# Last layer: picks 16 buffers ahead, rows brought back straight into their place, additions of four tiles; mixer: a unit's gates in one instruction

## The reference, cut to what matters

```python
x = x + 0.5 * ffn(layernorm(x), gate_w, experts)
x = x + mixer(layernorm(x), ...)
x = x + 0.5 * ffn(layernorm(x), gate_w, experts)

def ffn(x, gate_w, experts):                      # E = 8 experts, M = N // E = 256 tokens each
    gates = sinkhorn(einsum('bnd,de->bne', x, gate_w))          # 8 iterations
    vals, idx = top_k(swapaxes(gates, -1, -2), M)               # each expert picks its 256 tokens
    routed = x[b_idx, idx]                                      # (e, b, m, d)
    out = einsum('ebmd,edf->ebmf', routed, experts) * vals
    return zeros_like(x).at[b_idx, idx].set(out)                # the last expert that picked a token wins

def mixer(x, ...):      # inner = 512 channels, 16 states each
    x_ssm, res = split(x @ W_in.T)
    xc = silu(conv(x_ssm) + conv_b); delta = softplus(xc)
    h_t = exp(delta_t * A) * h_{t-1} + xc_t * xc_t              # a scan over 2048 tokens
    return (xc * sum(h) * silu(res) + D * xc) @ W_out.T
```

## Time and profile before

| | us |
|---|---|
| median of 3 runs | 3703.75 |
| lowest and highest run | 3695.53, 3709.73 |
| the profiled execution: its own time | 3714.21 |
| its span | 3712.6 |
| last stage (ffn), from 3294 us to the end | 418.6 |
| mixer, about 330 to 2950 us | 2620 |
| busy over the span: DVE, PE, ACT, POOL | 3117.0, 2790.2, 2127.8, 1321.5 |

### The profile page before, as it was taken

How to read it: one execution, slowest core, us unless ns; L and a number is a source line. 1 busy time by engine, 2 the same in 40 slices (tenths; PEclk the granted TensorE clock), 3 DMA queues, 4 the chain that set the end, 5 groups by cost and what they waited for, 6 DMA issues and landing times. The chain is left out here.

```text
span 3712.6 us, 29747 instructions
## 1 busy us (share of the span) xinstructions
PE 2790.2 (75%) x9252; PEld 1532.0 (41%) x9252; DVE 3117.0 (84%) x2640; ACT 2127.8 (57%) x2285; POOL 1321.5 (36%) x894
## 2 busy tenths in 40 slices
PE   8702688889889889988978978998897796035553
PEld 4501343345346345434534634543452455024442
DVE  6797479999999999999999999999999667982222
ACT  5300467876877877688687787778767362001111
POOL 0002265346245344534624534460111100036665
PEclk9655799999899899999989989998998896567776
DMA  6202278688778878867877787885676571034666
GB/s 265 117 0 80 68 174 182 142 174 181 156 167 165 178 163 179 193 134 170 182 161 170 160 178 162 175 193 119 126 150 132 113 283 81 0 117 145 206 220 241
DMA packets 146178, 575.61 MB, mean 155 GB/s; under 512 B 22096, under 2 KB 73872, under 8 KB 99216
## 3 DMA queue, kind: packets, MB, share of 16 engines
q0 software_dynamic: 76704, 400.61, 51.9%
q1 hardware_dynamic: 69360, 173.68, 12.6%
HBM read 154.72 MB, written 119.60 MB: 74 GB/s over the span
## 5 line engine op out<-in xcount | busy, mean ns | idle before, releaser
L1182 DVE TENSOR_TENSOR_SCAN state<-state,drive 128x2048 f32<-128x2048 f32 x512 | 2224.3, 4404 | 51.5 <-ACT state L1388 51.0
L1388 ACT ACTIVATE state<-delta,neg_a 128x2048 f32<-128x2048 f32 x512 | 1019.5, 2005 | 208.0 <-DMA delta<-xc 83.3
L1639 PE MATMUL ps_states<-state,ident 128*128 128x512 f32 x1792 | 847.5, 618 | 81.2 <-DMA state<-state 64.0
L1067 POOL DMA_DIRECT2D state<-state x255 | 235.7, 926 | 1306.1 <-DVE state L1182 1286.8
L1541 PE MATMUL ps_proj<-x1t,w_in 128*128 128x512 f32 x1024 | 515.9, 650 | 92.2 <-ACT res L1337 33.7
L1639 PEld LDWEIGHTS ps_states<-state,ident 128*128 128x128 f32 x1792 | 345.1, 198 | 481.4 <-issue 381.0
L1557 PE MATMUL ps_proj<-conv_in,tap 128*128 128x512 f32 x1024 | 487.8, 627 | 56.6 <-ACT conv_in L1301 35.3
L996 POOL DMA_INDIRECT picked<-normed_rows,slot_now x112 | 355.1, 3170 | 100.9 <-PE ps_rows L1522 56.0
L1541 PEld LDWEIGHTS ps_proj<-x1t,w_in 128*128 128x128 f32 x1024 | 207.2, 207 | 379.0 <-issue 276.7
L1012 POOL DMA_INDIRECT x<-routed_rows,row_now x112 | 344.2, 3074 | 34.8 <-issue 34.8
L1557 PEld LDWEIGHTS ps_proj<-conv_in,tap 128*128 128x128 f32 x1024 | 204.0, 202 | 321.7 <-issue 280.5
(11 more groups left out here) (298 smaller groups left out, 3253.1 us busy)
## 6 DMA issues: line engine op xcount, KB each, us to landing
state<-state POOLq DMA_DIRECT2D x255, 1024.0 KB, 7.1
delta<-xc POOLq DMA_DIRECT2D x24, 1024.0 KB
normed_rows<-rows_in SPq DMA_DIRECT2D x8, 2048.0 KB
x_rows<-x SPq DMA_DIRECT2D x16, 1024.0 KB, 7.7
normed_rows<-rows_mid SPq DMA_DIRECT2D x8, 2048.0 KB
f_total<-x_rows SPq DMA_DIRECT2D x8, 2048.0 KB
routed_rows<-f_routed SPq DMA_DIRECT2D x128, 128.0 KB
out<-f_total SPq DMA_DIRECT2D x8, 2048.0 KB
```

The costliest lines, as they stand in the source:

```text
L1067: nc.gpsimd.dma_start(out=state[held(q)][:], in_=state[held(q - 1)][:], accum_op=ALU.add).then_inc(pair_landed(b, q // 2)[0], 16)
L1182: nc.vector.tensor_tensor_scan(state[held(q)][:], state[held(q)][:], drive[j % 2][:], 0.0, ALU.mult, ALU.add).then_inc(state_ready, 1)
L1388: nc.scalar.activation(state[held(q)][:], delta[j % 2][:], ACT.Exp, scale=g.neg_a[:, j, n:n + 1]).then_inc(decay_ready, 1)
L1639: mm = nc.tensor.matmul(ps_sum[c][:], g.ident[:], state[held(q)][:, c * CH:(c + 1) * CH], start=(opening and n == 1), stop=(n == N - 1))
```

## The change

In `ffn`:

- NX and NY are 16 instead of 8. Picks and brought tiles take their indices from `slot_token` and `token_row` directly; the copies and the waits around them are gone.
- Brought tiles land in `rows`, two buffers of a whole batch (16 tiles), and wait for no addition. The first of a batch waits for the output store of two batches before and, as before, for the batch's 16 stores.
- Of brought tiles 4 go out per 5 picks (`rows_due`), from slot 23 on; what is left follows the last pick.
- DVE adds four tiles in one instruction (GROUP = 4), into `rows`, which is then stored. `added` counts groups.
- SP loads the experts one at a time, those from the third on after a turned slot each, then x of batch 0; x of batch 1 at slot 16; later ones behind the output store of two batches before (which starts five slots after a batch's last brought tile is due), without waiting for it to land. The last batch's output is stored in four parts.
- PE waits for each expert by itself.

In `mixer`: the four PSUM banks are one tensor; a unit's gates are one DVE instruction, 128x2048, for all units but the last; and three of the seven early picks go out after the first pair of the first batch instead of before it.

```diff
@@ mixer
-    ps_sum = [ps(f"ps_states{c}") for c in range(C)]
+    ps_states = ctx.enter_context(nc.psum_tensor("ps_states", [P, NT], F32))
+    ps_sum = [ps_states[:, c * CH:(c + 1) * CH] for c in range(C)]
...
-                for s in range(NX + 4 - FIRST_FFN):
+                for s in range(NX + 1):
                     pick(b + 1, s)
...
                     nc.gpsimd.dma_start(out=state[held(q)][:], in_=state[held(q - 1)][:], accum_op=ALU.add
                                         ).then_inc(pair_landed(b, q // 2)[0], 16)
+                if first and q == 1:
+                    for s in range(NX + 1, NX + 4):
+                        pick(b + 1, s)
...
-            for c in range(C):
-                if last:
-                    dve.wait_ge(end_summed, c + 1)
+            if not last:
+                nc.vector.tensor_tensor(gate_of[j][:], ps_states[:], gate_of[j][:], ALU.mult).then_inc(gated, C)
+            for c in range(C if last else 0):
+                dve.wait_ge(end_summed, c + 1)
@@ ffn
-    NX = NY = NK = 8
+    NX = NY = SL
     NT4 = 4
-    BRING, JOIN, LOAD = SL + 6, SL + 10, 3
+    GROUP = 4
+    NG = T // GROUP
+    BRING, STEP = SL + 6, 5
+
+    def rows_due(n):
+
+        return T * NB if n >= NB * SL else max(0, (n - BRING) * (STEP - 1) // STEP)
+
+    def slot_of(m):
+
+        return next(n for n in range(NB * SL + 1) if rows_due(n) >= (m + 1) * T)
...
-    back = [sb(f"f_back{i}", [P, D]) for i in range(NK)]
+    rows = [sb(f"f_rows{i}", [P, T, D]) for i in range(2)]
...
+        def load_x(m):
+            if m >= 2:
+                sp.wait_ge(added, (m - 1) * NG)
+            sp.dma_start(total[m % 2][:], x_v[m]).then_inc(x_in[m % 2], 16)
+
+        def store_out(m):
+            sp.wait_ge(added, (m + 1) * NG)
+            sp.dma_start(out_v[m], rows[m % 2][:]).then_inc(out_stored[m % 2], 16)
+
+        inside = [m for m in range(NB) if slot_of(m) + 5 < NB * SL]
         for e in range(E):
-            sp.dma_start(expert[:, e, :, :], g.experts[e].rearrange("(k p) f -> p k f", p=P)).then_inc(expert_in, 16)
+            if e >= 2:
+                sp.wait_ge(turned, (e - 2) * NH + 1)
+            sp.dma_start(expert[:, e, :, :], g.experts[e].rearrange("(k p) f -> p k f", p=P)).then_inc(expert_in[e], 16)
         load_x(0)
-        load_x(1)
-        rounds(turn)
...
+        for n in range(NB * SL):
+            b, s = n // SL, n % SL
+            sp.wait_ge(scaled, n + 1)
+            sp.dma_start(routed_v[b][s // NH, 1 + s % NH * P:1 + (s % NH + 1) * P, :],
+                         routed[s % NY][:]).then_inc(routed_out[s % NY], 16)
+            if n == SL:
+                load_x(1)
+            for m in inside:
+                if n == slot_of(m) + 5:
+                    store_out(m)
+                    load_x(m + 2)
+        for m in range(len(inside), NB - 1):
+            store_out(m)
+            if m + 2 < NB:
+                load_x(m + 2)
+        for q in range(NG):
+            sp.wait_ge(added, (NB - 1) * NG + q + 1)
+            sp.dma_start(out_v[NB - 1, :, q * GROUP:(q + 1) * GROUP, :],
+                         rows[(NB - 1) % 2][:, q * GROUP:(q + 1) * GROUP, :]).then_inc(out_stored[(NB - 1) % 2], 16)
...
+        def pick(b, s):
+            pool.wait_ge(turned, count(b * SL + s - NX + 1))
+            pool.sem_inc(g.passed_pool, 1)
+            nc.gpsimd.indirect_dma_start(
+                out=picked[s % NX][:], out_offset=None, in_=g.normed,
+                in_offset=bass.IndirectOffsetOnAxis(ap=g.slot_token[:, b, s:s + 1].bitcast(U32), axis=0)
+            ).then_inc(picked_in[s % NX], 16)
+
+        def bring(m, t):
+            if m == 0 and t == 0:
+                pool.wait_ge(table.ranked, 1)
+            if t == 0:
+                pool.wait_ge(out_stored[m % 2], m // 2 * 16)
+                for k in range(NY):
+                    pool.wait_ge(routed_out[k], (m + 1) * 16 * (SL // NY))
+            pool.sem_inc(g.passed_pool, 1)
+            nc.gpsimd.indirect_dma_start(
+                out=rows[m % 2][:, t, :], out_offset=None, in_=g.routed[m],
+                in_offset=bass.IndirectOffsetOnAxis(ap=g.token_row[:, m, t:t + 1].bitcast(U32), axis=0)
+            ).then_inc(back_in[m % 2][t // GROUP], 16)
+
+        for n in range(NB * SL):
+            pick(n // SL, n % SL)
+            for v in range(rows_due(n), rows_due(n + 1)):
+                bring(v // T, v % T)
...
+        def add_group(v):
+            m, q = v // NG, v % NG
+            part = slice(q * GROUP, (q + 1) * GROUP)
+            if q == 0:
+                dve.wait_ge(x_in[m % 2], (m // 2 + 1) * 16)
+            dve.wait_ge(back_in[m % 2][q], (m // 2 + 1) * 16 * GROUP)
+            nc.vector.tensor_tensor(rows[m % 2][:, part, :], rows[m % 2][:, part, :], total[m % 2][:, part, :], ALU.add
+                                    ).then_inc(added, 1)
+
+        def groups_due(n):
+
+            return rows_due(n - 2) // GROUP
...
-                if s == 1 and isinstance(b, int):
-                    pe.wait_ge(expert_in, E * 16)
+                if s and (s - 1) % NH == 0 and isinstance(b, int):
+                    pe.wait_ge(expert_in[(s - 1) // NH], 16)
```

More of the change, by code:

```diff
@@ L1845, in turn @@
                     dve.wait_ge(table.ranked, 1)
-                if s == 2 and there(b + 1):
-                    set_slots(b + 1)
-                m, t = behind(b, s, JOIN)
-                if there(m):
-                    if t == 0:
-                        dve.wait_ge(x_in[m % 2], (m // 2 + 1) * 16)
-                    dve.wait_ge(back_in[t % NK], (m * (T // NK) + t // NK + 1) * 16)
-                    nc.vector.tensor_tensor(total[m % 2][:, t, :], total[m % 2][:, t, :], back[t % NK][:], ALU.add
-                                            ).then_inc(added, 1)
-                if s == RANKED + 1 and there(b):
-                    set_rows(b)
-        set_slots(0)
         split_tokens(nc, g, dve, table)
-        rounds(turn)
+        for b in range(NB):
+            slots(b)
+        for v in range(groups_due(NB * SL), NB * NG):
+            add_group(v)
     @block.scalar
```

81 lines of the change are left out of this document (12 added, 69 removed).

## The result

The kernel after takes 3745.58 us (median of 4 runs, 3739.87 to 3762.21), the kernel before 3704.14 us (median of 4): a ratio of 1.0126, 95% interval 1.0103 to 1.0150. The forecast was 3653, range 3616 to 3700. The profiled execution took 3747.52 us, its span is 3746.0.

The account below looks back on a forecast made before the run. It took DVE to bound the mixer and POOL's gather issuing, with 66 us of pauses, the last stage. Terms -44 + 7 - 4 - 3 + 1 - 6 - 2 = -51 us gave 3653 us by the median, range 3616 to 3700.

Parts of the forecast that it names:

- I take 22 us left: Last stage: of POOL's 66 us of pauses between gathers, 22 remain with 16 buffers, a gain of 44 us.
- 6 us or more: Last stage: assumed time per slot while PE's hand-overs to DVE are late, against 2.25 us of POOL's gathers.
- the chain, not POOL, sets the pace: Rival, last stage: PE's hand-overs stay late while POOL issues, last pick no earlier; span 3714 to 3724 us; chance 0.14.
- up to 10 us: Last stage: POOL's exposed wait before batch 6's first brought row if the last slots' hand-overs are late; otherwise hidden.
- 2.85 us a slot: Chain rival's pace at which slots leave in the last stage, today's, from (3663.71 - 3346.30)/111.
- Held gathers, +7: Last stage: gathers starting beside DVE's longer four-tile additions are held, costing 7 us (0 to 13).
- Start, -4: Start of last stage: earlier first transposes as expert loads no longer crowd them, and dropped index copy; 4 us gained (0 to 6).
- End, -3 and +1: End of last stage: last output store in four parts gains 3 us; a longer last addition costs 1 us.
- Gates, -6, and first batch, -2: Mixer: 31 single-instruction gates gain 6 us (+2 to -9); moving three picks behind the first pair gains 2 (0 to -9).
- what its instructions cost there counts one to one: Mixer: DVE, busy 2359 of 2430 us, sets the pace, so time saved in its instructions shortens the kernel equally.
- Rival of the DMA engines: Last stage: DMA load rises from 62.5% to about 72%, 84% behind the last pick; adding 15 us gives 3668; chance 0.12.
- 66 us of pauses: Last stage of the kernel before: POOL's idle time beyond 1.25 us a gather, from first to last brought row.

Follow-up runs that it names:

- a2: Kernel after with picks only 4 slots ahead of PE instead of 16, in a group with late hand-overs: 3702.08 us, 1.0002 of the kernel before.
- s2: Kernel after plus a 0.55 us memset on POOL behind gathers from first brought row to last pick, POOL waiting for it: 3734.51 us, 1.0055 of the kernel before.
- g1: Kernel after with each four-tile addition made as four one-tile instructions, hand-overs on time: 3633.55 us, 0.9977 of the kernel before.
- r1: Kernel after, unchanged, run again in a group with on-time hand-overs: 3645.32 us, 1.0002 of the kernel before.
- m1: Mixer of the kernel after joined to the last layer of the kernel before, hand-overs on time: 3642.18 us, 0.9995 of the kernel before.
- h1: Kernel after with PE making only half of each expert product (8 weight loads and matmuls a slot, not 12), late hand-overs: 3720.12 us, 1.0047 of the kernel before.
- c1: Kernel after with one-tile additions, 32 pick buffers and first brought row after 31 picks, late hand-overs: 3759.80 us, 1.0155 of the kernel before.
- c2: As c1, plus two 8-column idle matmuls a slot and 2 product banks instead of 4, late hand-overs: 3810.45 us, 1.0287 of the kernel before.

## Why the prediction was wrong

**The step that failed** is "I take 22 us left": that 16 slots of buffer would take up late hand-overs, because "the hand-overs recover at each pause, which 16 slots still bring". I treated a late hand-over as a given delay that a deeper buffer hides. It is made by POOL's own dense issuing and grows for as long as that goes on: the 3-slot lead of the kernel before was what kept hand-overs under 12 us. With 16 slots the spells reach 15 to 17 us a slot, where the prediction reckoned with "6 us or more", and 29.7 us of lateness. There are fewer pauses, but long ones, 8 to 15 us before the first brought rows of batches 1 to 5, where the prediction had one of 8; 96.5 us of pauses instead of 66 or 22. a2 (the lead alone set back: no loss) and s2 (gathers spread: no lateness) show it from both sides.

**The rival "the chain, not POOL, sets the pace"** is what happened: last pick at 3661.90 where it said 3660, then 44 gathers. It gave 3714 to 3724 for the span, 3746 was measured. Against its 3714, the first brought row comes 18 us later (of the start it forecast 4 us less, 12.3 more were measured, and the mixer gave 6 instead of 8), the way from there to the last pick is 8 us shorter, and from the last pick to the end it is 84.1 us instead of 62. Of these 22 us, 17.3 are the wait at batch 6's first row: the "up to 10 us" for the output store of batch 4, which SP issues only behind slot 127's store, with the last slots as late as the others. (Its 2.85 us a slot is 3.02 by the rows, since 128 - 23 = 105 picks follow the first brought row and not 111; the sum doesn't use it.) It had 0.14; rows 4 deserved more, since the only argument against it leaned on pauses that the change removes.

**Held gathers, +7:** right in mechanism, and 4.3 in size. With additions by tile POOL's busy time is 10.6 us less (g1), and the whole is worth 9 us; against the kernel before, whose short additions hold gathers too, r1 has 259.5 - 255.2 = 4.3 us more.

**Start, -4:** the first transposes come 3295.06 - 3290.09 = 5.0 us after the first pick instead of 9.2, as said. It earned nothing in the profiled run: with the experts out of its way PE meets late hand-overs already in batch 0, and the first brought row comes 12.3 us later. On time, it comes 46.7 us after the first pick in r1 and 49.9 in m1: 3 us gained.

**End, -3 and +1:** -2.2 us. Right.

**Gates, -6, and first batch, -2:** the groups of the gates line, one gate and the scan behind it, and DVE's scans of the first batch in the kernel after (these answer to the earlier trace rows):

```profile
L1156 DVE TENSOR_TENSOR res<-ps_states,res x24: 2261/2265/2268, 549.9 to 2878.2; 128x2048 f32<-128x2048 f32 x24
...
549.89 2.27 DVE L1156 TENSOR_TENSOR res<-ps_states,res 128x2048 f32<-128x2048 f32 x1
552.07 4.42 DVE L1187 TENSOR_TENSOR_SCAN state<-state,drive 128x2048 f32<-128x2048 f32 x1
...
477.72 4.42 DVE L1187 TENSOR_TENSOR_SCAN state<-state,drive 128x2048 f32<-128x2048 f32 x1 [7.05 <-ACT state L1393]
485.67 13.05 DVE L1187 TENSOR_TENSOR_SCAN state<-state,drive 128x2048 f32<-128x2048 f32 x3 [3.53 <-ACT state L1393]
```

and, of the kernel before, the row behind the last one of the earlier trace rows:

```profile
492.68 8.74 DVE L1182 TENSOR_TENSOR_SCAN state<-state,drive 128x2048 f32<-128x2048 f32 x2 [1.05 <-ACT state L1388]
```

From a gate to the next scan it is now 552.07 - 549.89 = 2.18 us instead of 2.38: 31 x 0.20 = 6.2 us, as forecast. In the first batch the waits of 13.16 and 1.05 us became 7.05 and 3.53: 3.6 us. Where the change acts it gives 9.8 us, more than the 8 forecast. Yet m1 measured 1.8, between 5 less and 2 more. DVE waits more elsewhere: between its first and its last scan it idles 81.0 us in the trace of the kernel before and 85.4 in that of the kernel after, although the first batch's waits fell by 3.6. Its waits for PE's `ps_rows` go from 11.2 to 15.9 us. So "what its instructions cost there counts one to one" did not hold; how much of this is scatter between single traces is not settled.

**Rival of the DMA engines:** the 16 are busy 58% and 68% in the two windows where they were 61% and 71%. In r1, between 3346 and 3666 us, they are busy 72%, about what the rival feared, and nothing is lost. Wrong here.

**The baseline.** Without late hand-overs the terms that are left make 4.3 - 3 - 2.2 - 1.8 = -3 us, and r1 shows 1.0002: nothing. So the 66 us of pauses that the forecast wanted to win from exist, all but 7, only in runs with late hand-overs, and there a deeper lead doesn't buy them.

## What to carry to other kernels

When a wait's end coincides with an engine falling silent, as rows 4 said of POOL, ask whether that engine makes the lateness, before giving it a deeper buffer that lets it run on. Where it does, a short lead (4 or 6 slots here, not 16) or gathers spaced out bound the harm, at a price in the runs without it (20 us for 4 slots). Keep DVE's instructions short beside POOL's gathers. And take the kernel before once more at another time: a pause that is in one trace and not in the next is not the kernel's.

## What the runs showed of the hardware

**In one sort of runs PE's signals come late while POOL issues gathers 1.25 us apart, and not at 1.66 us** (s2, one trace); in a late spell that is under way a slot then takes 1.3 to 1.5 us for each weight load or matmul (h1, c1, c2). DVE's own signals stay prompt: PE starts 0.48 us after the start of the copy of 3382.88, 0.06 us after its end. So do ACT's: in the kernel before SP issues each of the 128 stores 0.03 us after the scaling that it waits for. It happened in three later groups of five and in the original runs, with one chip number in both sorts; in the other two groups gathers 1.25 us apart do nothing of the kind. What differs between the sorts, and by what path POOL reaches PE, stays open. Whether PE's work is done in time and only its signal is late, the traces can't tell either: the ends of matmuls in them are modelled. Load on the DMA engines alone is not it: they are busy 72% in r1, without late hand-overs, and 58% in the kernel after, with them. The Trainium skill has a mechanism of this form in "NOTIFIC — the notification-queue block", section "Overflow: three behaviours, one of which stalls the engine": records that instructions write pass through a shared block, and a full queue or internal FIFO there can hold back the engine that produces them. The section adds that the overflow marks were never seen set in its own measurements. The mechanism would make the cost go by instructions, as in h1, c1 and c2; no run here shows that it is at work. Not tried, and the next thing to try, is a spacing between 1.25 and 1.66 us: at 1.4 us, 232 gathers would pay, as an estimate, 232 x 0.15 = 35 us for what now costs the kernel before some 60.

**A four-tile addition costs more than its length:** 32 instructions of 1.22 us instead of 128 of 0.42 us take less of DVE and 9 us more of the whole, because a gather that starts beside one takes up to 1.9 us (g1 against r1). The Trainium skill, "SBUF — State Buffer", section "Who interferes with whom", agrees in part: it says that a DVE instruction with two inputs in SBUF, which these additions are, contends with a GpSimd instruction that reads SBUF, and the gathers take their indices from there. That the shared ports are held for the whole instruction it says of DVE's 2-port modes, a condition that the prediction left out. And it tells of a probe in which `tensor_tensor` did not stall DMAs; the 1.90 us gather beside an addition in r1 is another matter, and the measurement decides.
